# Taking the gate columns of the first chunk in the split matmul passes, with 35 warm-up matmuls in place of 24

## What is computed

```python
c = x @ W + (x @ lora_A[idx]) @ lora_B[idx]          # per tile, R = 16
result = c @ W_base.T + b_base                       # 512 x 512
logits = c @ W_gate.T                                # E = 8
h = einsum('bnd,erd->bner', c, A)                    # 8 experts x 16
out = x + result + einsum('bner,eor->bno', h * top2_softmax(logits), B)
```

## Time and profile before

| what | value |
|---|---|
| median of three runs | 65.09 us |
| profiled execution, its own time | 65.07 us |
| its span in the trace | 63.9 us |
| TensorE matmuls busy | 60.6 us, 95% of the span, 420 instructions |
| VectorE, ScalarE, GpSimd busy | 36.8, 25.6, 17.3 us |
| data moved | 8.46 MB, mean 133 GB/s |

### The profile page before, as it was taken

How to read it: one execution, slowest core, us unless ns; L and a number is a source line. 1 busy time by engine, 2 the same in 40 slices (tenths; PEclk the granted TensorE clock), 3 DMA queues, 4 the chain that set the end, 5 groups by cost and what they waited for, 6 DMA issues and landing times.

```text
span 63.9 us, 1272 instructions
## 1 busy us (share of the span) xinstructions
PE 60.6 (95%) x420; PEld 59.6 (93%) x420; DVE 36.8 (58%) x131; ACT 25.6 (40%) x73; POOL 17.3 (27%) x41
## 2 busy tenths in 40 slices
PE   4999999999999999999999999999999999999950
PEld 4979999999999999999999999999999999999940
DVE  0957699909899455110887758990477240477120
ACT  1761989325766080010172536511272011173620
POOL 1000799899988603020030301130000000000000
DMA  0799999604994002232323213630016000007044
GB/s 0 228 337 354 365 394 412 227 5 157 326 354 170 5 0 49 60 70 60 73 62 73 61 36 70 240 119 0 0 68 261 10 0 0 0 35 294 0 164 164
DMA packets 5048, 8.46 MB, mean 133 GB/s; under 512 B 1057, under 2 KB 1569, under 8 KB 5042
## 3 DMA queue, kind: packets, MB, share of 16 engines
q1 hardware_dynamic: 4370, 7.57, 36.1%
q0 software_dynamic: 384, 0.56, 2.5%
q10 hardware_dynamic: 288, 0.27, 1.2%
HBM read 5.26 MB, written 2.10 MB: 115 GB/s over the span
## 4 chain that ended last, share of the span: by engine, by line
PE 91%; DMA 4%; ACT 1%; issue 0%
PE bank L485 22%; PE bank L487 22%; PE bank L486 22%; PE bank L493 8%; PE bank L495 6%; DMA w_raw<-fold_in 4%; PE bank L571 3%; PE bank L536 2%; PE bank L552 2%; PE bank L542 2%; PE bank L578 1%; PE bank L582 1%; PE bank L526 1%; ACT y_out L331 1%
## 5 line engine op out<-in xcount | busy, mean ns | idle before, releaser
L485 PE MATMUL bank<-cl_hi,x_hi 128*128 128x408 f32 x32 | 11.4, 356 | 0.0
L487 PE MATMUL bank<-cl_hi,x_lo 128*128 128x408 f32 x32 | 11.2, 349 | 0.0
L486 PE MATMUL bank<-cl_lo,x_hi 128*128 128x408 f32 x32 | 11.1, 348 | 0.0
L485 PE MATMUL bank<-cr_hi,x_hi 128*128 128x256 f32 x32 | 9.6, 301 | 0.0
L486 PE MATMUL bank<-cr_lo,x_hi 128*128 128x256 f32 x32 | 9.0, 282 | 0.0
L487 PE MATMUL bank<-cr_hi,x_lo 128*128 128x256 f32 x32 | 9.0, 282 | 0.0
L259 POOL CAST cl_hi<-lora_raw 128x64 fp32r<-128x64 f32 x8 | 2.2, 281 | 16.9 <-PE bank L487 16.8
L446 DVE MAX8 top_val<-bank 128x8 f32<-128x8 f32 x8 | 1.4, 170 | 8.7 <-PE bank L536 8.7
L485 PEld LDWEIGHTS bank<-cr_hi,x_hi 128*128 128x128 f32 x32 | 6.1, 190 | 0.2
L226 POOL DMA_DIRECT2D lora_raw<-lora x8 | 4.5, 564 | 6.4 <-issue 6.3
L485 PEld LDWEIGHTS bank<-cl_hi,x_hi 128*128 128x128 f32 x32 | 6.0, 188 | 0.1
(11 more groups left out here) (97 smaller groups left out, 148.5 us busy)
## 6 DMA issues: line engine op xcount, KB each, us to landing
x_raw<-x_t SPq DMA_DIRECT2D x8, 256.0 KB, 4.1
out<-y_out SPq DMA_DIRECT2D x7, 256.0 KB, 2.1
w_raw<-fold_in SPq DMA_DIRECT2D x4, 256.0 KB, 4.8
w_raw<-fold_in SPq DMA_DIRECT2D x3, 324.0 KB, 4.9
bw_rows<-bw_hi SPq DMA_DIRECT2D x16, 40.5 KB, 2.0
lora_raw<-lora POOLq DMA_DIRECT2D x8, 64.0 KB, 3.2
bw_rows<-bw_lo SPq DMA_DIRECT2D x8, 40.5 KB, 2.1
ffn_b_raw<-ffn_b SPq DMA_DIRECT2D x1, 256.0 KB, 6.0
```

Source lines behind the costliest of these rows:

```text
L485: nc.tensor.matmul(out, a_hi, b_hi, start=first, stop=False, skip_group_check=True)
L486: nc.tensor.matmul(out, a_hi, b_lo, start=False, stop=False, skip_group_check=True)
L487: return nc.tensor.matmul(out, a_lo, b_hi, start=False, stop=last, skip_group_check=True)
```

## The change

The unsplit path goes. ScalarE casts the gate columns of chunk 0 first of all, TensorE waits for that cast too and takes all 392 left columns in each of chunk 0's three passes, and VectorE subtracts them together with the rest of the chunk. The late cast, the late subtraction and their wait are removed, and there are 11 more warm-up matmuls.

```diff
-WARM_UPS = 24
+WARM_UPS = 35
...
         def raw_wg(m):
-            return w_raw[:, m, D:][:, wg_cols(m)]
+            return w_raw[:, m, D:]
...
             act.wait_ge(w_first_loaded, DMA)
+            nc.scalar.copy(wg_hi[:, 0, 0:GH], raw_gh(0)).then_inc(gh0_hi_done, 1)
             for m in range(KC):
...
-            nc.scalar.copy(wg_hi[:, 0, 0:GH], raw_gh(0)).then_inc(gh0_hi_done, 1)
...
-                lo(wg_lo[:, m, wg_cols(m)], raw_wg(m), wg_hi[:, m, wg_cols(m)], w_lo_done)
-            dve.wait_ge(gh0_hi_done, 1)
-            lo(wg_lo[:, 0, 0:GH], raw_gh(0), wg_hi[:, 0, 0:GH], gh0_lo_done)
+                lo(wg_lo[:, m, :], raw_wg(m), wg_hi[:, m, :], w_lo_done)
...
             def fold_pass(m, w, wg):
-                cols = slice(GH, LEFT) if m == 0 else slice(0, LEFT)
+                cols = slice(0, LEFT)
...
-            pe.wait_ge(w_first_loaded, DMA)
-            for i in (3, 0, 1, 2):
-                if i == 0:
-                    pe.wait_ge(wa_loaded[0], DMA)
-                nc.tensor.matmul(bank[i][:, 0:GH], w_raw[:, 0, i * P:(i + 1) * P], raw_gh(0),
-                                 start=True, stop=False, skip_group_check=True)
             for m in range(KC - 1):
                 if m == 0:
+                    pe.wait_ge(gh0_hi_done, 1)
                     pe.wait_ge(w_hi_done, 1)
                     pe.wait_ge(wb_left_hi_done, 1)
                     for i in range(KC):
-                        nc.tensor.matmul(bank[i][:, GH:LEFT], wt_hi[:, 0, i * P:(i + 1) * P], wg_hi[:, 0, GH:LEFT],
-                                         start=False, stop=False, skip_group_check=True)
+                        nc.tensor.matmul(bank[i][:, 0:LEFT], wt_hi[:, 0, i * P:(i + 1) * P], wg_hi[:, 0, 0:LEFT],
+                                         start=True, stop=False, skip_group_check=True)
...
-            pe.wait_ge(gh0_lo_done, 1)
```

More of the change, by code:

```diff
@@ L114, in adaln_ffn_kernel @@
         w_hi_done, w_lo_done = sem("w_hi_done"), sem("w_lo_done")
-        gh0_hi_done, gh0_lo_done = sem("gh0_hi_done"), sem("gh0_lo_done")
+        gh0_hi_done = sem("gh0_hi_done")
         lb_hi_done, lb_lo_done = sem("lb_hi_done"), sem("lb_lo_done")
@@ L140, in raw_gh @@
             return w_raw[:, m, D:D + GH]
-        def wg_cols(m):
-            return slice(GH, WIDE) if m == 0 else slice(0, WIDE)
         def raw_wg(m):
-            return w_raw[:, m, D:][:, wg_cols(m)]
+            return w_raw[:, m, D:]
         def lb(t, h):
```

## The result

| | kernel before | changed kernel |
|---|---|---|
| median of 22 runs each | 65.50 us | 65.85 us |
| lowest to highest | 64.81 to 66.06 us | 65.47 to 68.41 us |
| profiled execution | 65.07 us, span 63.9 | 65.58 us, span 64.4 |

The ratio of the changed kernel to the one before is 1.0079, with a 95% interval from 1.0051 to 1.0107: slower by some 0.5 us. (Every ratio here leaves out the runs that lie over 1.5% above the fastest of their kernel; of the changed kernel's these are 66.58, 67.92 and 68.41 us.) The medians of all 22 runs differ by 0.35 us. The forecast was 65.3 us, 0.22 us slower, with a range up to 65.6. The sign was right; the size was too small, and the time lies outside the range.

A forecast was written before the change was run, and what follows sets the result against it. TensorE's unbroken stream was taken as the bound: 0.56 us gained by an earlier start, 0.71 paid for added columns and 0.08 for lag, so 0.22 us later, 65.3 us; 8-in-10 range 65.05 to 65.6.

The forecast's parts named there:

- The frame: TensorE is one unbroken stream from 3.75 us, so moving chunk 1's start (8.04) moves the end by the same amount.
- the lag behind the idle moment: At the first split matmul, filling after idle time adds 0.08 us, bounds 0 and 0.15.
- the gate cast is free: Chunk 0's gate cast takes 0.21 us of ScalarE, but VectorE's left cast still ends last, by 0.05 us.
- the start of the first split matmul: In chunk 0, at 4.66 us: VectorE's left cast ends at 4.61, plus 0.04 for the semaphore.
- the handing over: From the end of VectorE's left cast to TensorE's first split matmul: 0.04 us for the semaphore.
- the last of the three: VectorE's left cast, ending at 4.61, is the last of three casts the first split matmul needs, by 0.05 us.
- a fixed clock: TensorE's clock rises from 1.2 to 2.4 GHz at about 4.7 us, near where split work can first start.
- rival 1: Clock rises later than 4.66 us, so chunk 0's split work runs cold: over 0.5% slower; chance 0.17.
- an early rise gives this kernel nothing: In chunk 0, an early clock rise gains the changed kernel nothing; a late one costs up to 0.25 us.
- Rival 2: No difference: data typically comes earlier than profiled, or the start lag is absent; 65.1 to 65.2 us, chance 0.18.
- Rival 3: Counting only TensorE work, 1.47 us out and 0.71 in: over 0.5% faster, 64.3 us; chance 0.06.
- Rival 4: Split work stalls, such as on reads behind three engines' writes; a 0.25 us stall gives 65.5 us; chance 0.09.

The follow-up runs named there:

- gate_cast_dve: Changed kernel with the cast of chunk 0's gate columns moved from ScalarE to VectorE; median 65.64 us, ratio 1.0102 to the kernel before.
- wait_order: Changed kernel with TensorE's wait on VectorE's cast written first of the three, not last; median 65.98 us, ratio 1.0115 to the kernel before.
- raw_again: The kernel before, run again without an edit; median 65.18 us, ratio 0.9956.
- split_again: The changed kernel, run again without an edit; median 65.56 us, ratio 1.0033 to the kernel before.
- raw_warm27: The kernel before with 27 warm-up matmuls instead of 24; median 65.69 us, ratio 1.0023.
- raw_warm35: The kernel before with 35 warm-up matmuls instead of 24; median 65.92 us, ratio 1.0062.
- split_warm24: Changed kernel with 24 warm-up matmuls instead of 35; six runs from 65.47 to 67.60 us in two groups, no ratio taken.
- half_raw: Kernel before, with gate columns of row blocks 1 and 2 moved to the split passes, 3 and 0 left raw; median 65.65 us, ratio 1.0042.
- no_gate_cols: Changed kernel with TensorE leaving out chunk 0's gate columns, casts and waits kept; median 65.09 us, ratio 0.9952 to the kernel before.
- split_warm1: Changed kernel with one warm-up matmul instead of 35; median 67.08 us, ratio 1.0247 to the kernel before.

## Why the prediction was right in sign and wrong in size

**The frame held.** "What moves before chunk 1 moves the end": from chunk 1 to the last matmul it is 53.24 us after and 53.28 before. The passes grew by 0.235 us each, the lag behind the idle moment is 0.08 us at the high clock (4.86 to 5.11 less 0.18), the gate cast is free (gate_cast_dve), and the 11 warm-ups are out of the way (TensorE then idles until 4.86).

**The step that failed first: the start of the first split matmul.** I put 4.66 us; it was 4.89 in the changed kernel's first profile, and 4.84 to 4.95 in the five profiles that have the columns and the waits of the changed kernel in their order, so 0.18 to 0.29 later. Of the 0.35 us by which chunk 1 starts behind my 8.26 in that first profile, this is 0.23; 0.11 is the low clock of the first matmul.
- 0.1 us is the handing over, sized from VectorE's own next step, which is not the same thing: TensorE met the last of three waits in a separate instruction. wait_order shows it, and also that 0.06 of the 0.1 us can be had back by the order.
- 0.1 to 0.2 us is the third load. VectorE's cast started at 4.32 in the earlier trace rows, and at 4.40 to 4.64 in all eleven later profiles. I took one draw, the earliest of twelve, for a constant. The kernel before has slack there while its raw matmuls end later than that cast (5.22 for 4.61 in the earlier trace rows; none was left in raw_again); the changed kernel never has any, so it turned a covered wait into one on the path. I had called VectorE's cast "the last of the three" without pricing its scatter.

With both put right, and the clock as in the first profile, the loss is 0.22 + 0.1 us and a little for the load: 8.49 in split_again against 8.04 plus the 0.08 us by which its first load was later, so 0.37 us. That is 0.6%, over the bound of 0.5%.

**The second step that failed: a fixed clock.** I read the rise at 4.7 us from one profile and let it vary only to the late side, as rival 1. With it went the base of the sum: I took the median of three runs, 65.09 us, for the kernel's time, and its later sets have 65.45 to 65.53 (raw_again 65.18), which is most of the miss in absolute time. The profiles give the rise (from the spacing of matmuls or the length of weight loads) with TensorE always starting at 0.90 us:

| profile | clock up at | chunk 1 at |
|---|---|---|
| raw_again | by 3.9 | 7.81 |
| raw_warm27 | 4.15 | 8.47, waits for its load |
| gate_cast_dve | 4.3 | 8.50 |
| kernel before | 4.7 | 8.04 |
| split_again | by 4.8 | 8.49 |
| raw_warm35 | 4.85 | 8.52 |
| split_warm24 | by 4.9 | 8.58 |
| changed kernel | 5.15 | 8.61 |
| half_raw | 5.75 | 8.55 |
| wait_order | 5.9 | 9.03 |
| no_gate_cols | 6.45 | 8.47 |
| split_warm1 (one warm-up) | 8.5 | 10.11 |

An early rise speeds the raw matmuls, which start as soon as the first load is there, and gives nothing to the changed kernel, whose split work began at 4.84 at the earliest: gate_cast_dve at 4.3 and split_again at 4.8 have the same chunk 1. With the clock up early the loss is 8.49 - 7.81 = 0.68 us instead of 0.37. Then both kernels start their split work at the same time, 0.15 us behind VectorE's cast (4.86 and 4.90), the raw matmuls are all free, and the added columns are lost in full. That is the floor of the changed kernel, whose lowest time is 65.45 to 65.52 us in each of its five sets with 24 or 35 warm-ups (two of them with an edit of casts or waits), against 64.7 to 64.9 for the kernel before. I had written this down, as "an early rise gives this kernel nothing", but only for the changed kernel's own time: I took the other kernel's gain as contained in its median. Its three runs of 64.91 to 65.22 us, which I also used against the scatter of the clock, were a narrow draw of a spread from 64.7 to 66.2 in the later runs (with single runs at 66.8 to 67.3 above it). A late rise costs both kernels, each about half of the added cold time, so it shouldn't widen the difference; no profile of the kernel before with a late rise shows that. The two measured ratios, 1.0079 and 1.0033, are 0.52 and 0.22 us. The mechanisms give 0.37 to 0.68 us for rises up to 4.8 us: the first ratio lies within, the second doesn't, though its interval reaches 0.45 us. How often the clock rises early no run tells, so where between these the typical loss lies stays open.

**The clock's scatter.** The profiles with 24 warm-ups or more have the rise between 3.9 or less and 6.45 us, so 1.3 us either way or more. The Trainium skill, "TensorE: Matmul & The Clock Gate", Part 1, has it vary by 500 ns either way from run to run. The kind of the rule holds here, where my three runs spoke against it; its size doesn't, and the profiles decide. The page speaks of sustained matmuls, though, and TensorE pauses ahead of chunk 0 in all of these profiles but raw_warm35, where the rise was at 4.85 us.

**Rivals.** Rival 1 (late clock) is real and its price is right (half of the cold time: 3.6 us cold cost 1.6), but the loss doesn't need it: in split_again the clock was up in time, and chunk 1 still started at 8.49. Rival 2 (load earlier than in the profile) had the wrong sign: in all eleven later profiles it was later. Rival 3 (count of work alone) needed the first split matmul at 4.1 us or before, and it was never ahead of 4.84; raw_warm35 shows why the raw path was cheap: it costs something only when its cover is gone. Rival 4 (a stall at the first split matmul) came in a small form: the handing over takes 0.1 us more than I had, less than half its price, and by the order of the waits, not by reads behind three engines' writes.

**What stays open.** What the times at 67 to 68 us are in the changed kernel (2 of its 22 runs), in split_warm24 (4 of 6, from 66.95) and in half_raw (3 of 12). split_warm1 shows that a clock up only at 8.5 us gives 67.1, and the share grows as TensorE idles ahead of the split work; but no profile of such a run exists, so that is argued and not shown. The kernel before has such times too, one in each of its later sets (67.05 of 29 runs, 67.26 of 23, 66.83 of 17), so they aren't the change's alone. No kernel with the full result was found that beats the one before.

## What to carry to other kernels

Before you take work out of an engine's stream, ask what could run in its place. Here the work that filled a wait for data was free up to the end of the wait, whatever its cost per column, and the work put behind the wait was paid in full. A stream that begins earlier also collects whatever comes early by chance (a load, the clock); one that waits for the last of several loads takes the latest of them each time. Price such a start from the scatter of several executions, and look at which of several waits is written last.

## What the runs showed of the hardware

- The clock's rise came between 3.0 us or less and 5.5 us behind TensorE's first matmul, in eleven profiles of kernels with 24 to 35 warm-ups. Between two executions of the kernel before, with the rise 0.8 us apart, it moved chunk 1 by 0.23 us though the first load was 0.16 us later.
- With only one warm-up it came 3.6 us behind the first split matmul, and cost 1.6 us.
- A TensorE instruction behind three waits starts 0.15 us after the end of the instruction that it waits for last, if that wait is written last (seven profiles), and 0.05 us if it is written first (one profile, wait_order). At the next matmul 0.06 us of the difference is left.
- Loads issued at the same time landed 0.1 to 0.3 us apart between executions, and once chunk 1's 0.85 us.
